# One graph transformer layer on one core: the normalized key-value product folded into the output weight, and weight pieces placed later in VectorE's order

## What is computed

```python
edge_index = stack([src, dst])
xn = layernorm(x)                               # x: 1250 x 1024
x = x + graph(xn) + mix(xn)                     # first half
x = x + ffn(layernorm(x))                       # second half: 8 experts, 2 per token

graph: W = zeros(1024, 1024).at[row, col].add(w)   # 41250 edges
       xn @ W.T + bias
mix:   q, k, v = split(xn @ W_qkv)
       q, k = relu(rmsnorm(q) * qn_w), relu(rmsnorm(k) * kn_w)   # 16 heads of 64
       kv = k.T @ v ;  k_sum = sum over tokens of k              # per head
       out = (q @ kv) / (q @ k_sum + 1e-6)                       # linear attention
       out @ W_out + b_out
ffn:   top 2 of 8 experts by gate logits; swiglu(t @ w1 + b1) @ w2 + b2, weighted
```

## Time and profile before

| | |
|---|---|
| median of 3 runs | 1120.47 us (1119.83 to 1121.78) |
| the profiled execution | 1117.66 us, of which the span is 1115.9 us |
| TensorE busy | 948.5 us, 85% of the span |
| VectorE busy | 758.8 us, 68% |
| ACT busy | 302.0 us, 27% |
| GpSimd busy | 195.0 us, 17% |
| mean granted TensorE clock | 0.936 |

### The profile page before, as it was taken

One profiled execution on the slowest core, in us unless ns is written; L12 is line 12 of the kernel. 1 busy time (PEld: TensorE's weight loads), 2 busy tenths in 40 slices (PEclk: granted clock), 3 DMA queues, 4 the chain that ended last, 5 costly groups with the idle time before them and its releaser, 6 DMA issues.

```text
span 1115.9 us, 18538 instructions
## 1 busy us (share of the span) xinstructions
PE 948.5 (85%) x5609; PEld 590.9 (53%) x5610; DVE 758.8 (68%) x1231; ACT 302.0 (27%) x502; POOL 195.0 (17%) x220
## 2 busy tenths in 40 slices
PE   2526999999999989999788999999726989999993
PEld 1323666666666655555555666666524545555551
DVE  4889788888888889722777777776564545555551
ACT  0561222222222222533111121211101323333331
POOL 1133000000000010000323232223102233243321
PEclk9757899999999999999889999999957999999997
DMA  7544544333343331493135443535536996977553
GB/s 242 158 141 144 215 151 150 139 124 124 139 150 141 141 132 39 114 316 101 55 95 168 123 146 124 162 99 174 170 135 235 310 302 148 314 204 211 118 105 57
DMA packets 77814, 176.17 MB, mean 158 GB/s; under 512 B 24180, under 2 KB 39482, under 8 KB 73922
## 3 DMA queue, kind: packets, MB, share of 16 engines
q1 hardware_dynamic: 70001, 147.40, 39.3%
q0 software_dynamic: 7776, 28.32, 11.3%
HBM read 113.54 MB, written 62.67 MB: 158 GB/s over the span
## 4 chain that ended last, share of the span: by engine, by line
PE 21%; DVE 13%; DMA 8%; issue 6%; ACT 2%; POOL 1%; SPq 1%; DVEq 0%; POOLq 0%; ACTq 0%
PE windows L946 8%; PE bank L838 5%; DMA arena<-t_dram,arena 4%; DVE arena L1437 4%; DMA out_x<-arena 3%; PE bank L964 3%; PE bank L937 2%; PE bank L831 1%; PE windows L899 1%; DVE arena L1476 1%; DVE arena L1436 1%; DVE arena L1438 1%; DVE arena L1471 1%; ACT arena L1128 1%; PE windows L838 1%
## 5 line engine op out<-in xcount | busy, mean ns | idle before, releaser
L758 PE MATMUL bank<-arena 128*125 128x512 f16 x960 | 218.6, 385 | 0.0
L838 PE MATMUL bank<-arena 128*125 128x512 f16 x864 | 195.5, 384 | 1.8 <-POOL arena L616 1.8
L758 PEld LDWEIGHTS bank<-arena 128*125 (+1 forms) x960 | 130.0, 139 | 74.0 <-issue 5.1
L838 PEld LDWEIGHTS bank<-arena 128*125 (+1 forms) x864 | 118.5, 138 | 67.4 <-issue 3.0
L946 PE MATMUL windows<-arena 128*128 x648 | 149.4, 381 | 0.0
L814 PE MATMUL bank<-arena 128*128 128x416 f16 (+1 forms) x576 | 103.1, 338 | 0.0
L946 PEld LDWEIGHTS windows<-arena 128*128 128x128 f16 x648 | 63.6, 98 | 65.7 <-issue 1.3
L814 PEld LDWEIGHTS bank<-arena 128*128 128x128 f16 x576 | 55.5, 97 | 44.0
L964 PE MATMUL bank<-arena 128*128 x324 | 74.4, 379 | 2.3 <-DVE arena L1639 2.3
L1332 DVE TENSOR_TENSOR arena<-windows,arena 128x1024 f32 x49 | 59.8, 1220 | 22.1 <-issue 7.7
L616 POOL TENSOR_TENSOR arena<-arena 128x250 f32 (+1 forms) x40 | 27.1, 677 | 265.7 <-ACT arena L1109 265.7
(11 more groups left out here) (227 smaller groups left out, 1421.4 us busy)
## 6 DMA issues: line engine op xcount, KB each, us to landing
arena<-split_dram SPq DMA_DIRECT2D x56, 512.0 KB, 5.1
arena<-in_w_flat SPq DMA_DIRECT2D x22, 1024.0 KB, 6.4
split_dram<-arena SPq DMA_DIRECT2D x44, 512.0 KB, 3.7
arena<-in_w_flat SPq DMA_DIRECT2D x40, 256.0 KB, 3.6
split_dram<-arena SPq DMA_DIRECT2D x80, 128.0 KB, 2.3
arena<-in_x SPq DMA_DIRECT2D x20, 448.0 KB
arena<-in_w_qkv SPq DMA_DIRECT2D x8, 1024.0 KB, 6.4
t_dram<-arena SPq DMA_DIRECT2D x10, 448.0 KB
```

The lines of the kernel that those rows point to most:

```text
L758: mm = pe.matmul(bank[b][0:TT, :], xt[:, l, k, tok(i)], wkv[:, r, k, c0:c0 + 512], start=(k == 0 and n == 0), stop=(k == KT - 1 and n == 2))
L838: mm = pe.matmul(o[half][0:TT, :], a_[:, l, k, tok(i)], w_[:, r, k, c0:c0 + 512], start=(m == 0 and k == 0 and c == 0), stop=(m == 1 and k ...
```

## The change

Three things.

- VectorE's order in a key and value tile: weight piece 0 moves from behind graph sum 1 to behind value half 0 (ahead of graph sum 3), weight piece 1 from behind graph sum 2 to behind graph sum 3.
- Attention is written another way: since the normalizer of a head is a number per token and the key sum a number per dimension, `ut` holds relu(q) x qn_w x k_sum in 32 bits. A unit is then one 32-bit matmul with the 0/1 matrix `head_mask` for the denominator, and VectorE multiplies `ut` itself with the inverse. kv divided by k_sum is transposed on TensorE (`kv_turn`, in turn 0) and multiplied into the output weight (`wo_fold`, 16 products of 3 matmuls, in turn 3; ACT and VectorE write the halves back to `wo`).
- SP loads the low half of `wo` behind the last write of the graph weight, ahead of `wq` 3,1 and of `wg`, instead of behind the sums of squares. `qss` and `usq` lie elsewhere so that it may.

```diff
             def kv_tile(i):
                 k_half(i, 0)
                 accumulate(4 * i, 0)
-                piece_lo(1 + i, 0)
                 k_half(i, 1)
...
                 accumulate(4 * i + 1, 1)
+                v_half(i, 0)
+                piece_lo(1 + i, 0)
+                accumulate(4 * i + 2, 0)
                 piece_lo(1 + i, 1)
-                v_half(i, 0)
-                accumulate(4 * i + 2, 0)
                 v_half(i, 1)
                 accumulate(4 * i + 3, 1)
...
             sp.wait_ge(acc_out, 16 * 2 * KT)
+            load_wo(1)
+            load_wq(3, 1)
             load_wg()
-            load_wq(3, 1)
...
             sp.wait_ge(eps_mm, 3)
-            load_wo(1)
...
+            def kv_turn():
+                pe.wait_ge(kvn_ready, 1)
+                for p in range(PAIRS):
+                    mm = pe.transpose(bank[3 + p // 4][:, (p % 4) * P:(p % 4 + 1) * P], kvn[:, p, :], ident)
+                mm.then_inc(kvt_psum, 1)
+            def wo_fold(n):
+                k, half = divmod(n, 2)
+                if n == 0:
+                    pe.wait_ge(kvt_ready, 1)
+                    for hl in range(2):
+                        pe.wait_ge(wo_in[hl], 16 * N_PIECE_O)
+                if n >= 3:
+                    pe.wait_ge(m_done, n - 2)
+                for c, (l, r) in enumerate(((0, 0), (0, 1), (1, 0))):
+                    mm = pe.matmul(bank[3 + n % 3][:, :], kvt[:, l, k * P:(k + 1) * P], wo[:, r, k, half * 512:half * 512 + 512], start=(c == 0), stop=(c == 2))
+                mm.then_inc(m_mm, 1)
...
             def attend_unit(j, g, unit):
-                for at, w in ((0, kvb), (256, ksb)):
-                    for c, (l, r) in enumerate(((0, 0), (1, 0), (0, 1))):
-                        mm = pe.matmul(o[:, at:at + AW], w[l][:, j, :], ut[:, r, j, bass.ds(g * AW, AW)], start=(c == 0), stop=(c == 2))
-                mm.then_inc(at_mm, 1)
+                pe.matmul(bank[2 + j % 2][:, 0:AW], head_mask, ut[:, j, bass.ds(g * AW, AW)], start=True, stop=True).then_inc(at_mm, 1)
...
+            def fold_hi(n):
+                k, half = divmod(n, 2)
+                a_.wait_ge(m_mm, n + 1)
+                a_.activation(wo[:, 0, k, half * 512:half * 512 + 512], bank[3 + n % 3][:, :], ACT.Copy, scale=FOLD).then_inc(m_hi, 1)
...
-                    a_.activation(ut[:, 0, ...], bank[u % 3][:, 0:n], ACT.Relu, scale=qnw[...])
-                    a_.activation(u32[u % 2][:, 0:n], bank[u % 3][:, 0:n], ACT.Relu, scale=qnw[...]).then_inc(q_evac, 1)
+                    a_.activation(ut[:, 2 * t + h, a:a + n], bank[u % 3][:, 0:n], ACT.Relu, scale=ks_sum[:, 2 * t + h:2 * t + h + 1]).then_inc(q_evac, 1)
...
-                v.tensor_tensor(ut[:, 1, ...], u32[u % 2][:, 0:n], ut[:, 0, ...], ALU.subtract).then_inc(q_split, 1)
...
-                v.scalar_tensor_tensor(a, o[:, 0:AW], SX, a, ALU.mult, ALU.mult).then_inc(at_f, 1)
+                v.scalar_tensor_tensor(a, ut[:, j, bass.ds(g * AW, AW)], SQ, a, ALU.mult, ALU.mult).then_inc(at_f, 1)
```

More of the change, by code:

```diff
@@ L802, in _, with q_units @@
             kv_sums()
[L805 removed]
+            def kv_turn():
[14 more added lines that the diff above has]
+                mm.then_inc(m_mm, 1)
+            def q_units(t, groups=0, first=False, last=False):
                 for u in range(6):
@@ L818, in q_units, with graph_part @@
                         steps(KV_GROUPS + 6 * t + u, u % 2)
[L819 removed]
+                    if first and u == 2:
+                        kv_turn()
+                    if last:
+                        for n in folds(u):
+                            wo_fold(n)
+            q_units(0, 6, first=True)
             q_units(1, Q_GROUPS - 6)
[L821 to L822 removed]
+            q_units(2)
+            q_units(3, last=True)
             def attend_unit(j, g, unit):
[L825 removed]
                 pe.wait_ge(at_f, START + (max(unit - 1, 0) if isinstance(unit, int) else unit - 1))
[L827 to L834 removed]
+                pe.matmul(bank[2 + j % 2][:, 0:AW], head_mask, ut[:, j, bass.ds(g * AW, AW)], start=True, stop=True).then_inc(at_mm, 1)
+            def graph_part(i, o, half, a, b):
                 c0 = half * 512
@@ L857, in _ @@
                     i, half, k = ahead[j]
-                    mix_part(i, (bank[6:8], bank[0:2])[i], 0, half, k, k + 4)
-            for hl in range(2):
-                pe.wait_ge(wo_in[hl], 16 * N_PIECE_O)
+                    graph_part(i, (bank[6:8], bank[0:2])[i], half, k, k + 4)
             pe.wait_ge(at_done, START + PAIRS)
@@ L878, in mix_tile @@
                         attend_unit(2 + half, t + 1, PAIRS * (t + 1) + 2 + half)
-                    mix_part(i, bank[0:2], 0, half, 0, KT)
+                    graph_part(i, bank[0:2], half, 0, KT)
                 if h == 0:
@@ L885, in mix_tile @@
                         attend_unit(j, t + 1, PAIRS * (t + 1) + j)
-                    mix_part(i, bank[0:2], 1, half, 0, KT)
+                    attend_part(t, h, bank[0:2], half, 0, KT)
             def gate_tile(i, h):
@@ L1095, in q_turn @@
                             acc_part_hi(k)
-            q_turn(0)
+            q_turn(0, first=True)
             q_turn(1, split=True)
-            with a_.Fori(2, KT // 2) as t:
-                q_turn(t)
+            q_turn(2)
+            q_turn(3, last=True)
             a_.wait_ge(acc_out, 16 * 2 * KT)
@@ new lines, in key_sums, with kvt_lo, fold_lo @@
+                ins.then_inc(kvn_ready, 1)
+            def kvt_lo():
+                for b in range(2):
+                    c = slice(4 * b * P, 4 * (b + 1) * P)
+                    v.wait_ge(kvt_hi, b + 1)
+                    ins = v.tensor_tensor(kvt[:, 1, c], bank[3 + b][:, :], kvt[:, 0, c], ALU.subtract)
+                ins.then_inc(kvt_ready, 1)
+            def fold_lo(n):
+                k, half = divmod(n, 2)
+                c = slice(half * 512, half * 512 + 512)
+                v.wait_ge(m_hi, n + 1)
+                v.scalar_tensor_tensor(wo[:, 1, k, c], bank[3 + n % 3][:, :], FOLD, wo[:, 0, k, c], ALU.mult, ALU.subtract).then_inc(m_done, 1)
@@ L1419, in q_turn @@
                     q_unit(t, u)
-                    if first and u in (1, 3, 4):
-                        (kv_split, ks_hi, ks_lo)[u // 2]()
+                    if first and u == 3:
+                        kvt_lo()
                     if split and u >= 3:
@@ L1424, in q_turn @@
                             acc_part_lo(k)
-            v.wait_ge(kvb_zero, 5)
+                    if last:
+                        for n in folds(u):
+                            fold_lo(n)
+            key_sums()
             q_turn(0, 6, first=True)
             q_turn(1, Q_GROUPS - 6, split=True)
-            with v.Fori(2, KT // 2) as t:
-                q_turn(t)
+            q_turn(2)
+            q_turn(3, last=True)
             def attend_unit(j, g, unit):
```

142 lines of the change are left out of this document (76 added, 66 removed).

## The result

The changed kernel takes 1123.51 us (median of 20 runs, 1122.09 to 1126.13), the kernel before 1119.79 in the same session (20 runs, 1116.67 to 1124.3): ratio 1.0036, 95% interval 1.0027 to 1.0046. It is slower, by 3.7 us between the medians and by 4.0 us by the ratio.

What follows compares the result with a forecast made beforehand. TensorE bounds the query stage; VectorE's chain sets the key and value tile's new period. Terms -10.0 + 2.2 + 9.8 - 0.5 - 1.3 + 0.4 - 1.1 = -0.5 us gave 1120.0, range 1114 to 1125.

Steps and rivals of the forecast that it cites:

- the clock falls in the loop: Rival, mix loop: TensorE's longer wait for GpSimd is followed by half clock in all three rings, +3.3 us, 1123.3; chance 0.13.
- The weight pieces: Key and value stage: moving both pieces cuts the tile period from 29.99 to 28.9 us; stage -10.0 us.
- The last sums: End of key and value stage: last `kv_sums` wait grows to some 4.2 us and the clock falls, +2.2 us.
- The query stage: Products +10.4 and transposes +0.9 on TensorE, removed VectorE wait -1.5: +9.8 us; loads of `wo` and `wg` covered.
- The start of the mix stage: Seven attention units shorter by 0.19 us each, -1.3 us; multiplication meeting GpSimd passes, +0.4.
- The multiplication: VectorE, mix stage: with both inputs in SBUF it waits for a long GpSimd pass to end; +0.4 at start, absorbed in loop.
- The loop: Mix stage: two units shorter -0.4, one multiplication +0.1 per ring; three rings, one at half clock: -1.1 us.
- the clock holds: Rival: clock stays up at the last sums and in the loop, 1116.1 to 1117.8 us; chance 0.34.

Runs made afterwards that it cites:

- third-of-the-fold run: Changed kernel with one of the three matmuls in each of the 16 output-weight products (high x high only): 1117.4 us, ratio 0.9968 to the kernel before.
- filled kernel after: Changed kernel plus 12 unused matmuls ahead of the attention wait in each of four pairs of tiles: 1116.02 us, ratio 0.9961 to the kernel before.
- piece 1 at the end: Changed kernel with weight piece 1 behind graph sum 4 instead of ahead of value half 1: 1124.0 us, ratio 1.0039 to the kernel before.
- the move alone: Kernel before with only VectorE's new order of weight pieces in the key and value tile: 1111.34 us, ratio 0.9925.
- the fold alone: Changed kernel with VectorE's old order in the key and value tile, keeping the output-weight products and 32-bit attention: 1132.4 us, ratio 1.0115 to the kernel before.
- the operand in the bank: Changed kernel, VectorE's multiplication reading the attention unit's bank instead of `ut` (output differs, other experts chosen): 1142.6 us, ratio 1.0204 to the kernel before.

## Why the prediction was wrong

The forecast was 1120.0 us and no change; it came to 1123.5 and slower, inside the range. The rival "the clock falls in the loop" (1123.3, chance 0.13) is what happened. That its number fits to 0.2 us is partly luck: it put 2.2 us more than before into the loop (3.3 less the 1.1) and nothing behind it, and the profiled execution has 6.6 and 1.9.

- **The weight pieces** (-10.0): right. Period 28.9 forecast, 28.73 measured; VectorE's first instruction of a tile has no wait; the stage gave 11.0 (11.7 less the 0.7 ahead of it). TensorE's wait came at graph sum 1, not 3. The first tile's wait of 2.46 us is one of 0.79.
- **The last sums** (+2.2): right. 4.13 us of wait, then half clock; filling the wait gave 2.0 back.
- **The query stage** (+9.8, less 0.5 for the sums of squares): right. Measured +10.5, of which 1.7 are the clock's (1.2 in the sums, 0.5 in the first unit), so 8.8 against 9.3. The third-of-the-fold run shows the same from the other side. `wo` and `wg` weren't waited for.
- **The start of the mix stage** (-1.3 + 0.4): -1.8 to the first wait, then +0.7.
- **The multiplication**: right that it lasts as long as GpSimd's pass where they meet and that this is absorbed. That it costs 0.1 more every time, 0.6 of a ring, was not foreseen.
- **The loop** (-1.1): this is the step that failed. It was sized as "three rings, one of them at half clock". The text had the growth of the wait (3.3 us forecast, 3.44 measured; partly luck, since 0.57 of it came from the multiplication's operand and went away with it) and then trusted one row, a 3.37 us wait passed at full clock, to hold for the others. In the kernel after, none of four waits of 2.9 to 5.3 us passed at full clock. The rival's price of 1.7 us a fall held for the short falls (1.7 in the second ring) and was low for the long ones: the first ring's part of TensorE, to VectorE's L1529 at 620.22, was 17.2 us instead of 14.7. Put together, the falls (+5.9), the operand (three times 0.6) and the shorter units (three times -0.4) come to 6.5 of the 6.6. The loop is +6.6 in the profiled execution, and +1.9 more behind the fourth wait, which the sum had left out.
- **The forecast without that step.** The fold's own terms add up to 9.8 - 0.5 - 1.3 + 0.4 - 1.1 = +7.3 us, and 7.4 is what it costs where the loop's waits are filled; so what was missed is the clock. That the filled kernel after comes to 1116.0 us, near the 1116.1 of "the clock holds", is chance: its last sums and the two waits ahead of the loop still fell, and the same remedy puts the kernel before at 1117.8.

## What to carry to other kernels

Work taken off TensorE ahead of a wait that another engine sets isn't a saving: the wait grows, and the clock may fall behind it, so the step can cost more than it removed. Price every wait as long as one that fell in your own traces (here from 1.93 us on) as a fall, however one like it passed, and look for the work behind it, since that runs at half speed. Where such a wait can't be shortened, independent matmuls (useful ones first, unused ones otherwise) that fill most of it are nearly free: here 20 + 16 + 40 of them and the moved weight pieces took the kernel from 1121.1 to 1103.2 us.

## What was not expected of the hardware

- The clock behind a wait. Waits of 2.91 to 5.31 us: half clock behind all four of the loop. 2.88 us behind twelve unused matmuls: 1.00. 1.99 to 2.22 us behind eight: fell, at the loop's first wait in all four runs that had them; 1.69 behind ten: 1.00. At the last sums 1.93 us fell in two runs (with piece 1 at the end of the tile), and 1.93 to 1.94 passed in the three with the old order. 3.37 us passed in the kernel before, and in the move alone 2.07 us passed and 2.11 didn't (at 649.92 and 703.60 us). The length of the wait alone doesn't decide; what does wasn't settled.
- The falls in the loop came in two sizes. Added up over windows of 1 us as above, a fall took 1.4 to 1.7 us, or 2.9 to 3.05. The long ones are six of the sixteen behind the loop's waits in the kernel after, the fold alone, piece 1 at the end and the third of the fold, and none of the four with the operand in the bank.
- A VectorE multiplication with a second operand in SBUF instead of a bank starts 1.86 us behind the start of the reciprocal before it, instead of 1.75, at the same duration of its own (0.42 us); with the operand in the bank the 1.75 came back.
